# A two-layer transformer on one core: first attention in a new order with its norm in halves, final norm in three groups, the last pair's weight split moved ahead of a rotation

## The chip, the core and the metric

The kernel runs on one core of a Trainium2 chip. The metric is the device time of one execution in microseconds (us); less is better. Five engines work side by side, each through its own queue in order: TensorE (PE in the rows; PEld its weight loads), VectorE (DVE), ScalarE (ACT), GpSimd (POOL) and SyncE (SP), which here only issues DMAs. They wait for each other on semaphores.

## What is computed

Input x has 1024 rows of 512 columns. Four stages follow, each `x = x + f(layernorm(x))`:

```python
x = x + L0_attn(layernorm(x))   # one head of width 128, softmax over all 1024 keys
x = x + L0_ffn(layernorm(x))    # silu(h W1) * (h W3), times W2; each W = base + mean|w - base| * sign(w - base)
x = x + L1_attn(layernorm(x))   # latent attention, 32 heads, keys chosen by a top-128 index, causal
x = x + L1_ffn(layernorm(x))    # x W^T + bias + eight low-rank additions
```

All products are in float32 quality: each operand is split into a rounded part `_h` and the rest `_l`, and three products (l h, h l, h h) are summed.

## The kernel before

The rows stand in eight tiles of 128 (`xt(0)` to `xt(7)`), which stay on chip throughout. Each engine's program is written out by hand; small strings of steps such as `ATT_ORDER` or `PE_ORDER` set its order, and the same name may stand in the strings of several engines, each doing its share of that step.

**A norm.** VectorE takes the statistics of a tile (L1030), makes mean and variance, ScalarE takes the root (L721), VectorE refines its inverse in five small operations (`newton`, L1005) and scales the tile (`norm_scale`, L1046). TensorE transposes it (L1403), ScalarE copies the rounded part out (L725), VectorE subtracts for the rest (`norm_lo`, L1040). The first norm waits for all eight tiles of x, and then goes through all tiles in one pass. The last norm stands behind a meeting of all five engines (`meet`).

**Weights of the feed-forward layer.** 44 chunks come in through a ring of buffers: SyncE loads base and weight (L424, L425), GpSimd subtracts (L563), ScalarE takes sign and absolute value with a sum (L735, L737) and by that frees the slot. The ring has three slots for nine chunks, then four; the fourth is `row_bc`, which until then holds the attention's output bias. The first 28 chunks must be through before the step `O1` of the first attention ends, since the mean of their absolute values is taken there.

**First attention.** TensorE makes queries and keys (four groups of products, steps `u`), then the values of all eight tiles. In `ATT_ORDER`, S(i) is the scores of query tile i: products on TensorE, maximum on VectorE (L1129), exp on ScalarE (L766), there followed by one weight chunk. T(i) is the transpose of its probabilities: TensorE (L1461), two copies on ScalarE (L774), two subtractions on VectorE (L1137). O is the product with the values for four query tiles, Y(i) the output product of a tile and its addition into x (L1149). All four engines follow the same string.

**Head pairs.** The second attention runs 16 pairs of heads. Their weights are prepared ahead: ScalarE rounds (L893), GpSimd makes the rest (`split_pair`, P in `TAIL_ORDER`, L623), SyncE stores them. When all are stored and the first are loaded again, SyncE signals `hd_go`, for which VectorE waits before its first score. M, L (GpSimd) and R (ScalarE) rotate the first pair's queries. In a pair, S is again a score tile (16 of them; VectorE L1349, exp L966), C the reciprocals of two tiles (L1355), GpSimd scales the probabilities (L692), T is one of 24 groups of transposes (L1715, L972, L1361), V0 to V3 the products with the latent values, W the split of their sum (ScalarE L984, GpSimd L701), Y the output products of four row tiles. Each period does half of the row tiles for the pair before and its own; what is left of the last pair comes at the very end (`output`, `LAST_BANKS`), with eight additions and statistics.

**Final layer.** After the meeting: norm of eight tiles, per tile 12 products with the combined matrix `wfin`, bias added on GpSimd (L710), sum on VectorE (L1390), store.

## Time and profile before

| | us |
|---|---|
| median of 3 runs (lowest, highest) | 1475.95 (1475.61, 1476.82) |
| profiled execution, time | 1476.29 |
| profiled execution, span of its records | 1474.5 |
| TensorE busy, share of the span | 1327.4, 90% |
| VectorE busy | 1105.6, 75% |
| ScalarE busy | 832.5, 56% |
| GpSimd busy | 640.5, 43% |

The profile page lists busy time, 40 slices of the span, the chain of work that ended last, and the costliest groups. The trace behind it holds every instruction with its start, length and what ended the idle time before it. Busy shares are a mean over stages with different limits; what a change is worth is read from its own stage.

### The profile page before, as it was taken

The numbers are of one execution on the slowest core, as the hardware profiler recorded it, in microseconds if no ns is written. First come the engines' busy times: TensorE is split into PE (matmuls) and PEld (weight loads), VectorE is DVE, ScalarE is ACT, GpSimd is POOL, SyncE is SP. The second block draws the span as 40 slices with busy tenths as digits, with TensorE's granted clock in tenths as the row PEclk, the third lists the DMA queues.
The fourth block names the chain that finished last, engine by engine and source line by source line (L and its number), as shares of the span: only waits on it lengthen the run. The fifth ranks groups of instructions, "written<-read, shape, count | busy, mean of one in ns | idle before, by whom it ended". The sixth has DMA issues, their size and how long they took to land.

```text
span 1474.5 us, 21228 instructions
## 1 busy us (share of the span) xinstructions
PE 1327.4 (90%) x7144; PEld 1105.3 (75%) x7144; DVE 1105.6 (75%) x2233; ACT 832.5 (56%) x1813; POOL 640.5 (43%) x629
## 2 busy tenths in 40 slices
PE   2777999999989789998659999999999999999977
PEld 1656788888789677776348888888888888888866
DVE  5637434433548599999969998898898998898864
ACT  4554442222236556774557767666676767667631
POOL 3421120000027445645556555655666555555522
PEclk9978999999999999998669999999999999999988
DMA  6531220000022334754820000000000000000101
GB/s 217 177 100 51 70 81 0 1 19 1 17 81 64 102 75 122 227 181 140 269 95 14 1 28 28 28 28 28 28 16 12 28 27 28 28 27 15 51 29 58
DMA packets 83722, 95.59 MB, mean 65 GB/s; under 512 B 11680, under 2 KB 59296, under 8 KB 83104
## 3 DMA queue, kind: packets, MB, share of 16 engines
q1 hardware_dynamic: 83616, 94.24, 20.2%
q8 instruction: 59, 0.97, 0.3%
q14 instruction: 47, 0.39, 0.1%
HBM read 75.34 MB, written 18.87 MB: 64 GB/s over the span
## 4 chain that ended last, share of the span: by engine, by line
PE 68%; DVE 18%; ACT 4%; issue 4%; DMA 2%; POOL 2%; SPq 1%; DVEq 1%; ACTq 0%; POOLq 0%
PE ps L328 16%; PE ps L330 15%; PE ps L329 15%; PE ps L1715 8%; PE ps L1735 3%; DVE acc L1299 3%; PE ps L1734 3%; DVE top L1310 2%; DVE xn_l L1361 1%; DVE rop L1322 1%; DVE acc L1313 1%; DVE rop L1320 1%; DVE pm L1349 1%; DVE rop L1321 1%; PE ps L1430 1%
## 5 line engine op out<-in xcount | busy, mean ns | idle before, releaser
L692 POOL TENSOR_SCALAR pm<-pm,smx 128x128 f32<-128x128 f32 (+7 forms) x256 | 190.5, 753 | 214.6 <-DVE smx L1355 214.6
L966 ACT ACTIVATE pm<-pm,smx 128x128 f32<-128x128 f32 (+7 forms) x256 | 197.2, 772 | 39.8 <-DVE smx L1349 38.7
L1349 DVE CUSTOM_DVE_ANT_0 pm<-ps,mbias 128x128 f32<-128x128 f32 (+7 forms) x256 | 191.3, 752 | 34.0 <-PE ps L1715 13.1
L1715 PE MATMUL ps<-ident,pm 128*128 128x128 f32 x1152 | 176.2, 278 | 9.0 <-DVE xn_l L1361 3.5
L972 ACT ACTIVATE xn_h<-ps 128x512 fp32r<-128x512 f32 (+3 forms) x256 | 128.8, 513 | 86.0 <-PE ps L1715 82.9
L1361 DVE TENSOR_TENSOR xn_l<-ps,xn_h 128x512 fp32r<-128x512 f32 (+3 forms) x256 | 144.6, 587 | 26.6 <-ACT xn_h L972 25.6
L328 PE MATMUL ps<-latT_l,qc_h 128*128 128x512 f32 (+3 forms) x384 | 143.1, 373 | 20.5 <-DVE smx L1349 12.5
L1715 PEld LDWEIGHTS ps<-ident,pm 128*128 128x128 f32 x1152 | 133.4, 142 | 35.3 <-issue 12.3
L330 PE MATMUL ps<-latT_h,qc_h 128*128 128x512 f32 (+3 forms) x384 | 134.1, 349 | 0.0
L329 PE MATMUL ps<-latT_h,qc_l 128*128 128x512 f32 (+3 forms) x384 | 133.4, 347 | 0.0
L1299 DVE SCALAR_TENSOR_TENSOR acc<-ps,iw,acc 128x768 f32<-128x768 f32 (+4 forms) x105 | 87.1, 876 | 23.5 <-ACT ps L865 23.3
L328 PEld LDWEIGHTS ps<-latT_l,qc_h 128*128 128x128 f32 x384 | 73.2, 191 | 37.4 <-DVE smx L1349 13.0
L1734 PE MATMUL ps<-xn_l,v 128*128 128x512 f32 (+3 forms) x256 | 92.7, 368 | 1.6 <-DVE xn_l L1361 1.6
L659 POOL TENSOR_TENSOR rop<-rop 128x512 f32<-128x512 f32 x60 | 77.3, 1288 | 36.2 <-DVE rop L1322 36.2
L328 PE MATMUL ps<-xn_l,wc 128*128 128x512 f32 x224 | 91.7, 409 | 0.0
L1313 DVE MATCH_REPLACE8 acc<-top,acc 128x640 f32<-128x640 f32 (+4 forms) x112 | 89.7, 809 | 0.0
L330 PE MATMUL ps<-xn_h,wc 128*128 128x512 f32 x224 | 89.3, 398 | 0.0
L329 PE MATMUL ps<-xn_h,wc 128*128 128x512 f32 x224 | 89.2, 398 | 0.0
L563 POOL TENSOR_TENSOR wring<-wring,base 128x512 f32<-128x512 f32 (+1 forms) x36 | 47.8, 1332 | 95.3 <-DMA wring<-in_L_ffn_w 95.1
L1735 PE MATMUL ps<-xn_h,v 128*128 128x512 f32 (+3 forms) x256 | 88.4, 364 | 0.0
L865 ACT ACTIVATE ps<-ps 128x640 f32<-128x640 f32 (+4 forms) x112 | 74.0, 690 | 24.8 <-PE ps L330 24.5
L1310 DVE MAX8 top<-acc 128x8 f32<-128x640 f32 (+4 forms) x112 | 85.8, 813 | 0.1
(280 smaller groups left out, 3699.1 us busy)
## 6 DMA issues: line engine op xcount, KB each, us to landing
iwq_raw<-in_L_attn_idx_wq_w SPq DMA_DIRECT2D x48, 256.0 KB, 3.2
base<-in_L_ffn_mean_w SPq DMA_DIRECT2D x28, 256.0 KB, 2.8
wring<-in_L_ffn_w SPq DMA_DIRECT2D x24, 256.0 KB, 3.0
ow_raw<-in_L_attn_o_w SPq DMA_DIRECT2D x8, 512.0 KB, 3.9
xn_t<-in_L_attn_o_w SPq DMA_DIRECT2D x8, 512.0 KB, 4.0
wuvo<-pr_even SPq DMA_DIRECT2D x8, 512.0 KB, 4.9
wuvo<-pr_hl SPq DMA_DIRECT2D x8, 512.0 KB, 4.8
wuvo_h<-wuvo SPq DMA_DIRECT2D x16, 256.0 KB, 2.6
```

The lines of the kernel that those rows point to most:

```text
L328: pe.matmul(dst, lh, rl, start=start, stop=False)
L329: pe.matmul(dst, ll, rh, start=False, stop=False)
L330: return pe.matmul(dst, lh, rh, start=False, stop=stop)
L692: pool.tensor_scalar(pm[:, i % 4, 0:w], pm[:, i % 4, 0:w], smx[:, 32 + i:33 + i], 0.0, ALU.mult, ALU.add).then_inc(hd_p, 1)
L966: act.activation(pm[:, i % 4, 0:w], pm[:, i % 4, 0:w], ACT.Exp, bias=smx[:, i:i + 1], scale=-1.0, accum_out=smx[:, 16 + i:17 + i]).then_in ...
L972: act.activation(dst[:, 4 * c:4 * c + nk, tile(tq % 4)], ps[:, 4 + i % 2, 0:nk * P].rearrange("p (k s) -> p k s", k=nk), COPY).then_inc(hd ...
L1299: dve.scalar_tensor_tensor(acc_of(t), score(n, t), w, acc_of(t), ALU.mult, ALU.add)\
L1349: dve.tensor_tensor_reduce(out=pm[:, i % 4, 0:w], in0=two_banks(2 * (i % 2), w), in1=mbias[:, TRI[t]:TRI[t + 1]], scale=1.0, scalar=3.0 * BIG,
L1361: dve.tensor_tensor(dl[at], ps[:, 4 + i % 2, 0:nk * P].rearrange("p (k s) -> p k s", k=nk), f(dh[at]), ALU.subtract).then_inc(hd_lo, 1)
L1715: done = pe.transpose(ps[:, 4 + i % 2, tile(k)], pm[:, tq % 4, tile(4 * c + k)], ident[:])
L1734: pe.matmul(ps[:, 6, q], v, pl[:, k, q], start=k == 0, stop=False)
L1735: done = pe.matmul(ps[:, 6, q], v, ph[:, k, q], start=False, stop=k == nk - 1)
```

## The change

*First attention.* x's two halves have a semaphore each, and norm statistics, root and scales are done by halves (`first_norm`). The raw weights and the bias have buffers of their own (`attn_raw`, `bo_bc`), which overlap the third base buffer; chunks from 28 on wait until these have been read. The ring has four slots from the start. The split of the weight matrix is cut into four pieces between the second half's tiles; wo's split (W) and the bias additions (B) stand later. The value tiles (V) stand behind S1, their bias comes by a one-row product, their rounded part is copied by ScalarE. Each engine has a string of its own.

*Head start.* `P15` stands ahead of `M3`; ScalarE's `R3` stands behind the last mask conversions.

*End.* A period of its own for the last pair (`LAST_PE` and its like): A(i) is the previous pair's output product of row tile i, B(i) the last pair's, both ahead of V3; P15 is reciprocal and scale of the last query tile on VectorE; W0 stands behind T20 on ScalarE, not behind T22. The meeting is gone. The norm runs over tiles 0-1, 2-3, 4-7; tiles 6 and 7 are scaled on GpSimd.

```diff
-    _slot = _c % 3 if _c < ROW_FREE else (_c - ROW_FREE) % 4
+    _slot = _c % 4
-              "P8 F0 F1 P9 F2 F3 P10 P11 M0 P12 L0 M1 P13 L1 M2 P14 L2 M3 P15 L3".split()]
+              "P8 F0 F1 P9 F2 F3 P10 P11 M0 P12 L0 M1 P13 L1 M2 P14 L2 P15 M3 L3".split()]
-             "S0 S1 S2 T0 S3 T1 S4 T2 S5 T3 S6 O0 T4 Y0 Y1 S7 Y2 T5 Y3 T6 T7 O1 Y4 Y5 Y6 Y7".split()]
+ATT_PE = items("S0 S1 V0 V1 V2 V3 S2 V4 V5 V6 V7 T0 S3 T1 S4 T2 S5 T3 S6 O0 T4 S7 Y0 Y1 T5 Y2 T6 Y3 T7 O1 "
+               "Y4 Y5 Y6 Y7")
+ATT_ACT = items("S0 S1 C2 V0 C2 S2 C1 V1 T0 C1 T1 S3 T2 S4 C1 T3 S5 C1 S6 C3 O0 T4 C1 S7 T5 C1 T6 C1 T7 O1")
+ATT_DVE = items("S0 S1 W0 V0 S2 B0 V1 T0 S3 T1 S4 T2 S5 T3 S6 B4 O0 T4 S7 Y0 Y1 T5 Y2 T6 Y3 T7 O1 Y4 Y5 Y6 Y7")
+LAST_PE = """T9 S11 T10 V0 S12 T11 T12 S13 T13 V1 T14 S14 T15 S15 T16 T17 V2 T18 T19 A0 T20 A1 T21 A3 T22 T23 A2
+    B0 B1 B2 B3 V3"""
+LAST_DVE = """C4 S10 T8 T9 T10 S11 T11 V0 S12 T12 C5 S13 C6 T13 V1 T14 S14 T15 S15 C7 T16 T17 P15 T18 V2 T19 T20 T21
+    T22 T23"""
+LAST_ACT = """T10 T11 V0 T12 S11 S12 S13 T13 V1 T14 T15 S14 T16 T17 S15 T18 V2 T19 T20 W0 T21 T22 T23"""
+LAST_POOL = "S8 S9 S10 S11 S12 S13 S14 W0"
...
+            def first_norm(half):
+                c = slice(4 * half, 4 * half + 4)
+                dve.wait_ge(ld_x[half], 64)
+                for t in range(4 * half, 4 * half + 4):
+                    dve.bn_stats(stats[:, 6 * t:6 * t + 6], xt(t))
...
+            for t in range(4, NT):
+                norm_scale(0, t)
+                norm_lo(0, t - 1)
+                if t == 4:
+                    dve.wait_ge(ld_a, 80)
+                split(wqkv_h[:, t - 4, :], wqkv_l[:, t - 4, :], raw[:, t - 4, :])
...
+                if kind == "S":
+                    if i == 0:
+                        pe.wait_ge(at_qkv, 4)
...
+            pe.wait_ge(hd_x, 4 * (PAIRS - 1) + 2)
+            norm_tile(3, 0)
+            norm_tile(3, 1)
+            last_product(0)
             pe.wait_ge(hd_olo, 2 * PAIRS)
-            for i in range(4):
-                output(4 + i, PAIRS - 1, LAST_BANKS[i], False, True)
-            meet(pe, 1)
+            for t in range(4, NT):
+                products(t, PAIRS - 1, SUM_BANKS[t], True, True).then_inc(hd_y, 1)
+            norm_tile(3, 2)
+            norm_tile(3, 3)
+            last_product(1)
+            last_product(2)
+            last_product(3)
+            norm_tile(3, 4)
+            norm_tile(3, 5)
+            for t in range(4, NT):
+                last_product(t)
+                if t < 6:
+                    norm_tile(3, t + 2)
```

ScalarE's queue of before in the steps S3 to T2 of the first attention (`p` is the exp's output, `sgn` and `wring` or `row_bc` a weight chunk, `xn_h` the copies of the transposed probabilities):

```order
L766 ACTIVATE p,sm<-ps,sm 128x1024
L735 ACTIVATE sgn<-row_bc 128x512
L737 ACTIVATE row_bc,absum<-row_bc 128x512
L774 ACTIVATE xn_h<-ps 128x4x128 x2
L766 ACTIVATE p,sm<-ps,sm 128x1024
L735 ACTIVATE sgn<-wring 128x512
L737 ACTIVATE wring,absum<-wring 128x512
L774 ACTIVATE xn_h<-ps 128x4x128 x2
```

And the same engine now, from T0 to T3:

```order
L823 ACTIVATE xn_h<-ps 128x4x128 x2
L771 ACTIVATE sgn<-row_bc 128x512
L773 ACTIVATE row_bc,absum<-row_bc 128x512
L823 ACTIVATE xn_h<-ps 128x4x128 x2
L809 ACTIVATE p,sm<-ps,sm 128x1024
L823 ACTIVATE xn_h<-ps 128x4x128 x2
L809 ACTIVATE p,sm<-ps,sm 128x1024
L771 ACTIVATE sgn<-wring 128x512
L773 ACTIVATE wring,absum<-wring 128x512
L823 ACTIVATE xn_h<-ps 128x4x128 x2
```

Before, a chunk stood between each exp and the copies of the tile before; now copies and exps follow each other, with fewer chunks between.

GpSimd's queue of before at the last pair of the weight preparation (`pr_hl` is the split, the three rows ahead of it are M3, `qc_l` is L2 and L3):

```order
L666 TENSOR_TENSOR qc_l<-rop,qc_h 128x512
L678 TENSOR_TENSOR rop<-rop,cosq 128x512
L679 TENSOR_TENSOR rop<-rop,sinq 128x512
L682 TENSOR_TENSOR rop<-rop 128x512
L623 TENSOR_TENSOR pr_hl<-pr_out,pr_hl 128x1024
L666 TENSOR_TENSOR qc_l<-rop,qc_h 128x512
```

The same place now:

```order
L685 TENSOR_TENSOR qc_l<-rop,qc_h 128x512
L642 TENSOR_TENSOR pr_hl<-pr_out,pr_hl 128x1024
L697 TENSOR_TENSOR rop<-rop,cosq 128x512
L698 TENSOR_TENSOR rop<-rop,sinq 128x512
L701 TENSOR_TENSOR rop<-rop 128x512
L685 TENSOR_TENSOR qc_l<-rop,qc_h 128x512
```

The split stands three operations earlier.

TensorE's queue of before at the last transposes of the last pair (`ident,pm`), with the last row of V2 ahead and the first of V3 behind:

```order
L1735 MATMUL ps<-pTa_h,v3 128x128
L1715 MATMUL ps<-ident,pm 128x128 x21
L1734 MATMUL ps<-xn_l,v3 128x512
```

The same place now, down to A3 (`wuvo` rows are output products, three of them for each of A0, A1, A3):

```order
L1871 MATMUL ps<-pTa_h,v3 128x128
L1851 MATMUL ps<-ident,pm 128x128 x6
L345 MATMUL ps<-wuvo_l,ol_h 128x512
L346 MATMUL ps<-wuvo_h,ol_l 128x512
L347 MATMUL ps<-wuvo_h,ol_h 128x512
L1851 MATMUL ps<-ident,pm 128x128 x4
L345 MATMUL ps<-wuvo_l,ol_h 128x512
L346 MATMUL ps<-wuvo_h,ol_l 128x512
L347 MATMUL ps<-wuvo_h,ol_h 128x512
L1851 MATMUL ps<-ident,pm 128x128 x3
```

Output products stand between the groups of transposes, where 21 transposes stood in a row.

## Rows read from the trace of the kernel before

**Rows 1.** The page: its span, and the chain that ended last by engine.

```profile
span 1474.5 us, 21228 instructions
...
PE 68%; DVE 18%; ACT 4%; issue 4%; DMA 2%; POOL 2%; SPq 1%; DVEq 1%; ACTq 0%; POOLq 0%
```

**Rows 2.** Windows: length, five engines' busy time (count), TensorE clock, DMA share, GB/s.

```profile
4.00:5.00 1.00, 0.00 (x0) 0.00 (x0) 0.00 (x0) 0.00 (x0) 0.00 (x0) 1.00 0.90 303
```

**Rows 3.** Timeline from the start: start, length, engine, line, operation, count, idle before.

```profile
0.73 3.71 SPq L396 DMA_DIRECT2D x<-in_L_attn_x  x8
...
9.40 4.84 DVE L1030 BATCH_NORM_STATS2 stats<-x 128x6 f32<-128x512 f32 x8 [9.40 <-DMA x<-in_L_attn_x]
...
15.20 3.91 POOL L563 TENSOR_TENSOR wring<-wring,base 128x512 f32<-128x512 f32 x3 [13.51 <-DMA wring<-in_L_ffn_w]
...
27.49 1.51 DVE L1046 TENSOR_SCALAR xn_t<-x,mv,rs_out 128x512 f32<-128x512 f32 x1
...
42.79 4.90 DVE L1073 TENSOR_TENSOR x<-x,row_bc 128x512 f32<-128x512 f32 x8
...
42.85 0.77 PE L328 MATMUL ps<-xn_l,wqkv_h 128*128 128x512 f32 x1 [9.63 <-DVEq L1071]
```

**Rows 4.** TensorE in the first attention (timeline), and the window 68 to 128.

```profile
56.56 0.22 PE L328 MATMUL ps<-wqkv_l,xn_h 128*128 128x128 f32 x1
...
67.23 0.45 PE L328 MATMUL ps<-qkT_l,qkT_h 128*128 128x512 f32 x1
...
76.30 1.91 PE L1461 MATMUL ps<-ident,p 128*128 128x128 f32 x8
...
101.28 0.79 PE L328 MATMUL ps<-xn_l,v_h 128*128 128x512 f32 x1 [4.09 <-DVE xn_l L1137]
...
127.49 0.80 PE L328 MATMUL ps<-xn_l,v_h 128*128 128x512 f32 x1 [1.41 <-DVE xn_l L1137]
...
68.00:128.00 60.00, 38.44 (x149) 29.46 (x148) 29.51 (x49) 37.61 (x71) 19.38 (x16) 0.76 0.36 118
```

**Rows 5.** One step of the first attention on ScalarE and VectorE (timelines).

```profile
84.18 1.12 ACT L766 ACTIVATE p<-ps,sm 128x1024 f32<-128x1024 f32 x1 [2.23 <-DVE sm L1131]
...
87.01 1.08 ACT L774 ACTIVATE xn_h<-ps 128x512 fp32r<-128x512 f32 x2
...
87.64 1.29 DVE L1137 TENSOR_TENSOR xn_l<-ps,xn_h 128x512 fp32r<-128x512 f32 x2 [3.50 <-ACT xn_h L774]
88.85 1.21 DVE L1129 TENSOR_REDUCE sm<-ps 128x1 f32<-128x1024 f32 x1
```

**Rows 6.** The start of the heads: ScalarE, GpSimd, VectorE (timelines).

```profile
742.54 1.06 ACT L893 ACTIVATE pr_hl<-pr_out 128x1024 fp32r<-128x1024 f32 x1
...
747.45 2.36 POOL L623 TENSOR_TENSOR pr_hl<-pr_out,pr_hl 128x1024 fp32r<-128x1024 f32 x1
...
754.55 0.29 DVE L1349 CUSTOM_DVE_ANT_0 pm<-ps,mbias 128x128 f32<-128x128 f32 x1 [6.10 <-issue]
```

**Rows 7.** The end: the window 1411 to 1425, then timelines of four engines.

```profile
1411.00:1425.00 14.00, 10.45 (x40) 8.20 (x41) 4.69 (x9) 5.20 (x11) 3.38 (x3) 0.63 0.01 2
...
1411.37 0.19 ACT L966 ACTIVATION_READ_ACCUMULATOR pm<-pm,smx 128x1 f32 x1
...
1411.85 2.11 POOL L692 TENSOR_SCALAR pm<-pm,smx 128x896 f32<-128x896 f32 x2 [4.90 <-DVE smx L1355]
...
1418.87 0.79 PE L1734 MATMUL ps<-xn_l,v 128*128 128x512 f32 x1 [1.56 <-DVE xn_l L1361]
...
1440.34 0.20 DVE L1009 RECIPROCAL rs_out<-rs_sqrt 128x8 f32<-128x8 f32 x1 [1.64 <-ACT rs_sqrt L721]
...
1441.59 1.00 DVE L1046 TENSOR_SCALAR xn_t<-x,mv,rs_out 128x512 f32<-128x512 f32 x2
...
1442.29 1.94 PE L1403 MATMUL ps<-ident,xn_t 128*128 128x128 f32 x8 [9.08 <-DVE xn_t L1046]
...
1449.15 0.60 PE L1403 MATMUL ps<-ident,xn_t 128*128 128x128 f32 x4
...
1470.86 0.40 PE L330 MATMUL ps<-qc_h,xn_h 128*128 128x512 f32 x1
```

More of the change, by code:

```diff
@@ L989, in _ @@
                 head_period(period)
-            meet(act, 1)
-            sqrt(6, NT)
-            for t in range(NT):
+            act.activation(table[:, 3:4], ones[:, 0:1], ACT.Sqrt)
+            sqrt(6, 2)
+            sum_half(PAIRS - 1, 3)
+            norm_hi(3, 0)
+            sum_hi(PAIRS - 1, 1)
+            norm_hi(3, 1)
+            sqrt(7, 2, 2)
+            norm_hi(3, 2)
+            norm_hi(3, 3)
+            sqrt(8, 4, 4)
+            for t in range(4, NT):
                 norm_hi(3, t)
@@ new lines, in half_norm @@
+                rsqrt(k, n, first)
+            raw = attn_raw[:, 0:NK * 3 * D0].rearrange("p (k n) -> p k n", k=NK)
+            def first_norm(half):
+                c = slice(4 * half, 4 * half + 4)
+                dve.wait_ge(ld_x[half], 64)
+                for t in range(4 * half, 4 * half + 4):
+                    dve.bn_stats(stats[:, 6 * t:6 * t + 6], xt(t))
+                dve.drain()
+                for t in range(4 * half, 4 * half + 4):
+                    dve.bn_aggr(mv[:, t, :], stats[:, 6 * t:6 * t + 6])
+                dve.drain()
+                dve.tensor_scalar(rs_var[:, c], mv[:, c, 1], EPS, None, ALU.add)
+                dve.drain().then_inc(at_rv, 1)
+                dve.wait_ge(at_rs, half + 1)
+                root(4, 4 * half)
@@ L1074, in _ @@
-            dve.drain().then_inc(row_free, 1)
             for u in range(4):
@@ L1080, in _, with values @@
                 dve.drain().then_inc(at_qkv, 1)
-            for b in range(2):
-                dve.wait_ge(at_proj, 5 + b)
-                tmp = xn_t[:, b, :].rearrange("p (k s) -> p k s", k=4)
-                for i in range(4):
-                    dve.tensor_tensor(tmp[:, i, :], ps[:, 4 + b, tile(i)], bv_bc[:], ALU.add)
-                dve.drain()
-                split(v_h[:, 4 * b:4 * b + 4, :], v_l[:, 4 * b:4 * b + 4, :], tmp)
-                dve.drain().then_inc(at_v, 1)
+            def values(b):
+                dve.wait_ge(at_vhi, b + 1)
+                dve.tensor_tensor(v_l[:, 4 * b:4 * b + 4, :], ps[:, 6 + b, :].rearrange("p (k s) -> p k s", k=4),
+                                  f(v_h[:, 4 * b:4 * b + 4, :]), ALU.subtract).then_inc(at_v, 1)
             def means(m, a, b):
@@ L1113, in row_stats @@
                 dve.bn_stats(stats[:, 6 * i:6 * i + 6], xt(i))
-            for kind, i in ATT_ORDER:
+            for kind, i in ATT_DVE:
+                if kind == "V":
+                    values(i)
+                    continue
+                if kind == "W":
+                    split(wo_h[:], wo_l[:], attn_raw[:, NK * 3 * D0:])
+                    dve.drain().then_inc(at_w, 1)
+                    continue
+                if kind == "B":
+                    for t in range(i, i + 4):
+                        dve.tensor_tensor(xt(t), xt(t), bo_bc[:], ALU.add)
+                    dve.drain().then_inc(at_b, 1)
+                    continue
                 if kind == "O" and i == 1:
@@ L1393, in _ @@
+            last_add(6)
+            last_stats(6)
+            last_add(7)
+            last_stats(7)
+            half_norm(8, 4, 4)
+            norm_scale(3, 4)
+            norm_scale(3, 5)
+            dve.drain().then_inc(en_rs, 1)
+            for t in range(NT):
+                if t < 4:
+                    norm_lo(3, t + 4)
+                last_out(t)
         @block.tensor
@@ L1682, in _, with products, output @@
                         queries(0, i)
-            def output(i, p, bank, first, last):
-                for q in ((p - 1, p) if not first and not last else (p,)):
-                    one = mm3(pe, ps[:, bank, :], ol_h[:, q % 2, tile(i)], ol_l[:, q % 2, tile(i)],
-                              wuvo_h[:, q % 2, :], wuvo_l[:, q % 2, :], q == p - 1 or first or last, q == p)
-                one.then_inc(hd_y, 1)
+            def products(i, q, bank, start, stop):
+                return mm3(pe, ps[:, bank, :], ol_h[:, q % 2, tile(i)], ol_l[:, q % 2, tile(i)],
+                           wuvo_h[:, q % 2, :], wuvo_l[:, q % 2, :], start, stop)
+            def output(i, p, bank):
+                if p:
+                    products(i, p - 1, bank, True, False)
+                products(i, p, bank, p == 0, True).then_inc(hd_y, 1)
             def head_period(period):
-                for kind, i, p in steps(PE_ORDER, period):
+                for kind, i, p in steps(LAST_PE if period == PAIRS - 1 else PE_ORDER, period):
                     if kind == "S":
```

341 lines of the change are left out of this document (203 added, 138 removed).

## The prediction

> **What bounds the kernel now.** I read the page's chain of work first [rows 1]: TensorE holds 68% of it and VectorE 18%, so over most of the span a cheaper instruction elsewhere gains nothing. The change touches neither the feed-forward weights nor fifteen of the sixteen head pairs, so I looked only at the stretches that it rewrites: the first attention (0 to 150 us), the start of the heads (743 to 755 us) and the end (from 1411 us).
>
> At the start VectorE waits until 9.40 us for all eight row tiles of x. The roots and scales that follow share their time with GpSimd's weight differences: a scale of one row tile that meets one takes 1.51 us, where two that meet none take 1.00 [rows 3, 7]. TensorE begins its projections at 42.85 us, when all of VectorE's weight splits are done. The 48 projection products take until 56.56 us, and the 96 narrow products of the values until 67.23 us, when the first scores begin [rows 3, 4].
>
> From there to 127.49 us, where the second output product begins [rows 4], no engine is full. A step repeats every 6.15 us, and it is a ring through two in-order queues [rows 5]: exp at 84.18, 1.3 us with its accumulator; one weight chunk (sign and abs) of 1.4 to 1.5 us, until the copies at 87.01; then ScalarE's first copy of the transposed probabilities, 0.6 us; VectorE's two subtractions 1.29 us; only behind them the next maximum, 1.21 us and some 0.3 us to the next exp. VectorE's queue holds T(i) ahead of S(i+1), and ScalarE's holds S(i) and a chunk ahead of T(i), though the scores of S(i+1) have long been computed.
>
> At the head start VectorE ends its top-k work at 748.45 us and takes the first score at 754.55. The signal that it waits for comes behind the last pair's store, and that store behind GpSimd's split, which starts at 747.45 though its input was complete at 743.60 [rows 6].
>
> At the end TensorE waits for the last probabilities, runs the last value product V3 at the lower of its two levels (granted clock 0.63 over 1411 to 1425), ends 36 output products at 1433.2, stands idle for 9.08 us until 1442.29 and ends at 1471.3 [rows 7]. That idle time is eight additions with statistics on VectorE, a meeting of all engines, a table load and the root.
>
> **Prices.** From 1449.15 to 1471.26 stand 84 wide products and 24 transposes [rows 7]; with 0.11 us a transpose, as a narrow product costs 10.67/96 [rows 4], a wide product is 0.23 us. The 48 projections took 13.7 us where 48 x 0.23 is 11.0, so one restart from the 1.2 GHz level costs 2.7 us. A VectorE root takes 1.25 us (1440.34 to 1441.59), a scaled row tile 0.5, statistics of a tile 0.6 (4.84/8) [rows 3, 7]. The three changes are far apart in time, with bound stretches between, so their gains add.
>
> **Part 1, the first attention.** *Halves.* Cumulating the 303 KB/us of DMA traffic from 2.0 us [rows 2], 1.05 MB are through at 5.4; with the 1.1 us by which the signal for all of x came behind its bytes, the first half is there at 6.5 (bounds: that, and 9.4 if the tiles land together). Four statistics, root and scales follow, the first scale at 11.1 instead of 19.45. GpSimd now has four ring slots free at once and works from 15.2 to 20.4. The second half's root ends at 22.0, after four tiles whose ring (scale, transposes, copy, subtraction) takes about 1.4 to 2 us each. The weight split is cut into four pieces of 0.4 + 0.55 us set between tiles 4 to 7, wo's split and the eight additions of the bias (4.90 us) go behind the scores. By hand the last subtraction ends at 31.8. To it I add collisions: a scale that met GpSimd took 1.51 us, not 0.5 [rows 3]; two of these make 33.5. Bounds: none 31.8; four and the late landing 38. Projections thus start 9.3 us earlier.
>
> No row shows VectorE's statistics beside a busy GpSimd, and the second four (17.3 to 19.7) will meet it. I take them at 0.6; were all four blocked like the scale, 4 us more, which the upper bound holds. The Trainium skill, SBUF — State Buffer, "SBUF: two separate sides", has the shared port pair as an exclusive lock that a VectorE instruction takes only in a two-port mode or with two SBUF inputs; by that rule statistics, with one input, would not be blocked. It speaks against the split pieces (a copy, and a subtraction of two SBUF inputs) set beside GpSimd's chunks: by it each of the eight could wait for one 1.3 us difference, half of it on average, and the projections would start at 37 instead of 33.5, the time being 3.5 us longer. The scale's 1.51 us agrees with the rule; no row here shows statistics beside GpSimd.
>
> *A new wait.* The scores S0 now stand straight behind the projections, ahead of the value tiles. TensorE ends the fourth projection at 33.5 + 13.7 = 47.2, ScalarE copies (0.7), VectorE splits (1.3), so S0 starts at 49.3 where the values used to hide that. Behind the 2 us wait I charge a restart: S0 and S1 take 5.1 us, to 54.4. Values V0 to V3 (5.8 us with the new bias product, which replaces four VectorE additions), S2 (1.4) and V4 to V7 (5.8) bring TensorE to 67.4, which is T0's start. Meanwhile the first three exps and five chunks run beside it. T0 began at 76.30 before: 9 us gained so far.
>
> *The steps.* ScalarE's new queue takes T(i) ahead of S(i+2), and its chunks no longer stand in each step. Hand-walking all three queues with the durations above gives T1 at 69.7, T2 at 72.1, T3 at 74.7 and the first output product at 78.8 (101.28 before). It ends at 84 to 87; ScalarE reaches it at 86.3, held by exp S6 and three chunks. Then T4 at 87, S7's exp at 91.5, T5 92, T6 94.1, T7 to 98.4 and its last subtraction at 100.2. ScalarE's own content from T0 is 8 x 1.08 + 5 x 1.3 + 9 chunks x 1.4 + 1.2 = 29 us, so 33 us is close to what that queue allows. I take 101.0 with a little lower clock: gain **26.5** (127.49 to 101.0). Bounds: 31 with no restart; if the lower level rules half of the steps (T + S costs 4.4 us there against 2.35) and the ring of two copies sets each step at 4.5 us, 18; with the late landing as well, 14. Behind this point the order is the old one.
>
> **Part 2, head start.** The split of the last pair moves ahead of the three rotation operations M3 (3.7 us). It waits for ScalarE's 743.60 and, behind L2, starts at 743.7 and ends at 746.05. Store, loads and drain are unchanged at 4.74 us (749.81 to 754.55), so VectorE starts at 750.8, behind its own 748.45. The table load of exp now stands behind R3, which waits for M3 (749.9), and ends near 751.9, so the first exp comes 0.8 us later behind its score than before; the first reciprocals have that slack. Gain **3.5**, bounds 2 (exp counts in full, and the two stores touch) and 3.75.
>
> **Part 3, the end.** The reciprocal and scale of the last query tile move to VectorE: exp ends at 1411.56, P15 is 1.2 us (1.00 as for two 512-column scales, plus a reciprocal), so it is done at 1412.8, against 1413.96 on GpSimd. The price: T18's subtraction and V2's addition wait behind it, and W0, now behind T20 on ScalarE, waits for that addition until 1414.25. So T21 to T23 are copied from 1414.9 and V3's input is complete at 1417.3. TensorE fills the gap: the output products of tiles 0, 1 and 3 (2.1 us) among the transposes, then A2 and B0 to B3 (3.5 us) from 1415.85 to 1419.3, then V3 at the full level, 3.0 us, to 1422.3 (some 1424.5 before, 36 products ahead of 1433.2). Here the filled gap must keep the clock up; if not, 2.7 us.
>
> Next the norm in groups of 2, 2 and 4. Tiles 0 and 1 have their sums at 1418.1 and 1419.4, their root at 1422.3, and the first scale at 1422.9. The last half-sum, tile 1's scale, the addition of tile 2 and tile 0's low part share VectorE, so the first final product starts at 1425.6. That gap has 1.2 us of work in 3.3, as the one before V3 had, so I charge a restart (2.7). Then 12 + 12 products (5.5), transposes of tiles 2 and 3 (0.9) and 36 products (8.25) run to 1442.95; the last four tiles' sums, statistics, root and first scale end at 1442.6 beside it, so little wait is left: tile 4's transposes, copy and low part end at 1445.0. The remaining 48 products and the 8 transposes of tiles 6 and 7 are 11.9 us, so TensorE ends at 1457.0, against 1471.26. Store and last addition behind it stay 3.25. Gain **14.3**. Bounds: 16.5 with no restart; 8 with restarts at V3 and again at tile 4.
>
> **Sum.** 26.5 + 3.5 + 14.3 = 44.3. The profiled execution took 1476.29 with a span of 1474.5; it gives 1432.0, and as the median of the runs shown is 0.34 lower, **1431.7 us**.
>
> **Rivals.** (1) *The lower clock and the queue ring keep half of the steps' gain.* For it: the mean granted clock over the old steps is 0.76, half of 68 to 128 us at the lower level [rows 4]. Against: gaps shrink. Attention then gives 14 instead of 26.5: 1444. (2) *The halves of x land together and GpSimd collides at every piece.* The start loses 4 us: 1435.5. (3) *The clock stays at its upper level*, since all three gaps are shorter: 2.7 at S0, 2.7 at the final norm, 2 in the steps: 1424.5. (4) *Slower: the weight ring becomes the bound.* A slot's round trip is issue 0.8, landing 3.0, difference 1.3, sign and abs 1.4 = 6.5 us, for four slots 1.6 us a chunk, and 28 chunks must be through before the second output product. It decides from (101 - 17.7)/28 = 3.0 us a chunk, a round trip of 12. If loads that now collide with more chunks in a row made it 19, chunks would end at 150.7 and the kernel, 23.2 behind the old point with 17.8 of other gains, at 1481, slower. The highest DMA share seen leaves no room for a threefold landing. (5) *The change doesn't do what it says*, an engine waiting for another's moved signal so that all stays as it was: 1476.
>
> **How the numbers follow.** Forecast 0.60, rival 1 0.18, rival 2 0.10, rival 3 0.08, rival 4 0.03, rival 5 0.01. The range 1422.5 to 1447 takes in rivals 1 to 3 and leaves out the tails of their bounds. A measurement of this kernel can tell 0.2% (3 us) from no change: faster 0.96, same 0.01, slower 0.03.
>
> **What would show it.** Right: the projections start near 33.5 us, the second output product near 101, VectorE's first score of the heads some 4 us less behind its last top-k replacement (2.4 us, not 6.1), V3 behind five product blocks, and TensorE's idle time between 1433 and 1442 gone. Wrong: ScalarE waiting for GpSimd's differences in the steps, a granted clock of 0.5 over most of 50 to 100 us, or TensorE idle for over 3 us ahead of tile 4's transposes.

## The result, and the profile after

The changed kernel takes **1443.72 us** (median of 4 runs, 1442.61 to 1445.15) against 1476.38 before: a ratio of 0.978, with a 95% interval of 0.976 to 0.980. The forecast was 1431.7 with a range of 1422.5 to 1447.0: the sign and the range held, and the time came out 12 us above the forecast. The profiled execution took 1442.61 us with a span of 1440.8, so the span lost 33.7 us where 44.3 were forecast.

```profile
span 1440.8 us, 21299 instructions
PE 71%; DVE 16%; ACT 4%; issue 3%; DMA 2%; POOL 1%; SPq 1%; DVEq 0%; ACTq 0%
```

The chain of work is TensorE's and VectorE's as in [rows 1]. Cut at the two points that the prediction used, the second output product and VectorE's first score, the 33.7 us come from these places:

| stretch | before, us | after, us | gain | forecast |
|---|---|---|---|---|
| to the second output product | 127.49 | 113.43 | 14.1 | 26.5 |
| from there to VectorE's first score | 627.06 | 623.55 | 3.5 | 3.5 |
| from there to the end of the span | 719.95 | 703.8 | 16.1 | 14.3 |

The miss lies in the first attention, 12.4 us short; the last stretch gave 1.8 more than forecast. TensorE's timeline of the changed kernel there (start, length, line, operation, output and inputs, count, idle time before and who ended it):

```profile
33.17 0.77 PE L345 MATMUL ps<-xn_l,wqkv_h 128*128 128x512 f32 x1 [2.17 <-DVEq L1143]
49.68 0.50 PE L345 MATMUL ps<-qkT_l,qkT_h 128*128 128x512 f32 x1 [2.71 <-DVEq L1149]
...
52.62 0.48 PE L1539 MATMUL ps<-bv_bc,ones 1*128 1x128 f32 x2
54.52 0.48 PE L1539 MATMUL ps<-bv_bc,ones 1*128 1x128 f32 x2
...
67.52 0.79 PE L1539 MATMUL ps<-bv_bc,ones 1*128 1x128 f32 x2
...
71.00 0.79 PE L1539 MATMUL ps<-bv_bc,ones 1*128 1x128 f32 x2
...
77.81 1.93 PE L1584 MATMUL ps<-ident,p 128*128 128x128 f32 x8
...
113.43 0.80 PE L345 MATMUL ps<-xn_l,v_h 128*128 128x512 f32 x1 [1.41 <-DVE xn_l L1214]
```

The projections start at 33.17 us (forecast 33.5, before 42.85), and S0 at 49.68 (49.3). But the transposes T0, forecast at 67.4 and at 76.30 before [rows 4], start at 77.81: the 9 us gained at the start are lost in the value tiles. L1539 is the product of one row of ones with the bias row that opens each value tile. A tile has 12 other products of 0.111 us, 1.33 us; it takes 1.90 (52.62 to 54.52), so the bias product costs 0.57 us where I charged 0.11. At the end a tile takes 3.48 us (67.52 to 71.00). The windows of the same stretch show why (us; then the busy time and instructions of PE, PEld, DVE, ACT and POOL; the granted clock; DMA share; GB/s):

```profile
50.00:54.00 4.00, 4.00 (x23) 3.14 (x21) 2.51 (x3) 3.74 (x7) 0.80 (x2) 1.00 0.73 230
54.00:58.00 4.00, 4.00 (x32) 3.62 (x32) 3.07 (x3) 3.62 (x8) 3.72 (x3) 1.00 0.49 167
58.00:62.00 4.00, 4.00 (x20) 3.71 (x20) 0.00 (x0) 1.43 (x5) 1.43 (x2) 0.61 0.77 241
...
74.00:78.00 4.00, 4.00 (x18) 3.66 (x18) 0.00 (x0) 0.00 (x0) 0.00 (x0) 0.50 0.02 4
```

The granted clock is 1.00 to some 58.8 us, then 0.5, the 1.2 GHz level, for 24 us, **while TensorE is busy all the time**: PE shows 4.00 of 4.00 us in each of these windows. Ahead of every fall in the profile of before TensorE had been idle a few microseconds earlier.

The start was as forecast. VectorE's second four statistics take 2.46 us, 0.6 each, with GpSimd's differences running from 15.63 to 20.86 beside all of them; what meets GpSimd and does wait is the split of q and k behind the projections, 1.62 to 1.68 us a subtraction instead of 0.69:

```profile
15.63 3.94 POOL L582 TENSOR_TENSOR wring<-wring,base 128x512 f32<-128x512 f32 x3 [13.95 <-DMA wring<-in_L_ffn_w]
17.34 2.46 DVE L1120 BATCH_NORM_STATS2 stats<-x 128x6 f32<-128x512 f32 x4
...
46.61 1.68 DVE L1086 TENSOR_TENSOR qkT_l<-xn_t,qkT_h 128x512 fp32r<-128x512 f32 x1
...
48.90 0.69 DVE L1086 TENSOR_TENSOR qkT_l<-xn_t,qkT_h 128x512 fp32r<-128x512 f32 x1
```

At the head start VectorE's first score comes 1.4 us behind its last top-k replacement, where it came 6.1 us behind before [rows 6]; the table load of exp (737.34) is now what the first exp waits for. At the end TensorE fills the gap ahead of V3, and the 9.08 us of idle time of [rows 7] are gone:

```profile
729.84 2.35 POOL L642 TENSOR_TENSOR pr_hl<-pr_out,pr_hl 128x1024 fp32r<-128x1024 f32 x1
734.41 1.21 DVE L1390 MATCH_REPLACE8 acc<-top,acc 128x1024 f32<-128x1024 f32 x1
736.98 0.29 DVE L1429 CUSTOM_DVE_ANT_0 pm<-ps,mbias 128x128 f32<-128x128 f32 x1 [1.36 <-issue]
...
1394.63 0.75 DVE L1442 TENSOR_SCALAR pm<-pm,smx 128x1024 f32<-128x1024 f32 x1
1398.72 1.29 DVE L1449 TENSOR_TENSOR xn_l<-ps,xn_h 128x512 fp32r<-128x512 f32 x2 [0.38 <-ACT xn_h L1030]
...
1402.02 0.39 PE L1870 MATMUL ps<-xn_l,v 128*128 128x512 f32 x1
...
1408.63 0.47 PE L345 MATMUL ps<-qc_l,xn_h 128*128 128x512 f32 x1 [0.71 <-DVE xn_l L1097]
...
1425.36 0.50 PE L345 MATMUL ps<-qc_l,xn_h 128*128 128x512 f32 x1 [0.98 <-DVE xn_l L1097]
```

V3 (from 1402.02) and the final products (from 1408.63) run at the upper level: no window behind 1388 us shows less than 1.00.

### The profile page after: what moved, and what is told of

It reads as the page before. It is cut to its first block, busy times and chain, and to the rows that moved or that the text cites. A ratio compares the mean times of both kernels' runs of the same rounds, so it can differ in the third digit from the quotient of the medians.

```text
span 1440.8 us, 21299 instructions
## 1 busy us (share of the span) xinstructions
PE 1329.5 (92%) x7160; PEld 1107.8 (77%) x7160; DVE 1107.4 (77%) x2247; ACT 832.9 (58%) x1819; POOL 641.7 (45%) x630
## 4 chain that ended last, share of the span: by engine, by line
PE 71%; DVE 16%; ACT 4%; issue 3%; DMA 2%; POOL 1%; SPq 1%; DVEq 0%; ACTq 0%
PE ps L345 17%; PE ps L347 16%; PE ps L346 16%; PE ps L1851 9%; PE ps L1871 3%; PE ps L1870 3%; DVE acc L1376 3%; DVE top L1387 2%; DVE xn_l L1449 1%; DVE rop L1399 1%; DVE acc L1390 1%; DVE rop L1397 1%; DVE pm L1429 1%; DVE rop L1398 1%; PE ps L1551 1%
## 5 line engine op out<-in xcount | busy, mean ns | idle before, releaser
L717 POOL TENSOR_SCALAR pm<-pm,smx 128x128 f32<-128x128 f32 (+1 forms) x255 | 188.8, 749 | 208.5 <-DVE smx L1436 208.5
L582 POOL TENSOR_TENSOR wring<-wring,base 128x512 f32<-128x512 f32 (+1 forms) x33 | 43.1, 1309 | 108.4 <-DMA wring<-in_L_ffn_w 108.1
L345 PE MATMUL ps<-ikT_l,iqT_h 128*128 128x512 f32 (+3 forms) x176 | 66.1, 376 | 23.3 <-DVE acc L1376 22.1
```

Of the source, the lines that this page charges most:

```text
L345: pe.matmul(dst, lh, rl, start=start, stop=False)
L717: pool.tensor_scalar(pm[:, i % 4, 0:w], pm[:, i % 4, 0:w], smx[:, 32 + i:33 + i], 0.0, ALU.mult, ALU.add).then_inc(hd_p, 1)
```

## The experiments

All build on the changed kernel, or on it with one edit, as said. They were taken on several chips, each beside the kernel of before, whose medians there were 1474.6 to 1476.4 us and whose single runs reached from 1470.0 to 1479.0; so a difference of 1 or 2 us between medians below says little by itself. Two theories were open on the 10.4 us that T0 came late. **A:** the bias products bring the clock down, beside their own price. **B:** the 2.7 us wait ahead of S0 does, and the products only cost their time.

### No bias product

```diff
 def value_tile(t):
     dst = ps[:, 6 + t // 4, tile(t % 4)]
-    pe.matmul(dst, ones[0:1, :], bv_bc[0:1, :], start=True, stop=False)
     for k in range(NK):
         last = mm3(pe, dst, xn_h[:, k, tile(t)], xn_l[:, k, tile(t)],
-                   wqkv_h[:, k, tile(2)], wqkv_l[:, k, tile(2)], False, k == NK - 1)
+                   wqkv_h[:, k, tile(2)], wqkv_l[:, k, tile(2)], k == 0, k == NK - 1)
```

> Leaves out the bias of the values: the product of one row of ones with the bias row, that opened each value tile, is gone, and the tile's first real product opens it; nothing else is changed. In the changed kernel a value tile took 1.90 us at the upper level (12 narrow products are 1.33), the clock fell at 58.7 us, and the first transposes T0 came at 77.8 us. Theory A, the bias products bring the clock down: eight times 0.57 us go and the clock stays up, S0 and S1 2.9, V0 to V3 5.3, S2 1.4, V4 to V7 5.3 behind 49.7 give T0 at 64.6, 13 us earlier; kernel 1430.5 to 1433. Theory B, the 2.7 us wait ahead of S0 brings it down and the products only cost their own time: the fall stays near 58.7, T0 comes near 71, kernel 1437 to 1439.

Measured 1429.56 us (1428.14 to 1431.64), a ratio of 0.969 (0.966 to 0.971) to before. T0 starts at 68.64, not at 64.6, because the wait ahead of S0 was 5.0 us in this run and the clock was low behind it until some 57 us; from there it stays at 1.00 up to 101. The time is below theory A's figure, and theory B's 1437 is out. A wait ahead of S0 does cost a restart, but the clock then comes back.

### The values first

```diff
-ATT_PE = items("S0 S1 V0 V1 V2 V3 S2 V4 V5 V6 V7 T0 S3 ...
+ATT_PE = items("V0 V1 V2 V3 S0 S1 S2 V4 V5 V6 V7 T0 S3 ...
```

> TensorE computes the value tiles V0 to V3, bias products and all, ahead of the first scores S0, so that they fill the 2.7 us in which it waited for the split of q and k; every other queue is as in the changed kernel. Theory A, the bias products bring the clock down: the wait goes but the clock still falls within some us of the first value tiles, T0 near 75 instead of 77.8, kernel 1440 to 1442. Theory B, the wait brings it down: no fall, the 19.5 us of S0 to V7 at the upper level stand straight behind 46.9, T0 near 66.5, kernel 1432 to 1434.

Measured 1436.28 us (1433.32 to 1439.79), T0 at 73.09. There is no idle time ahead of the first value tile, and the clock falls all the same, inside V2; it comes back in the scores and falls again inside V6:

```profile
46.00:50.00 4.00, 4.00 (x30) 3.54 (x30) 3.21 (x4) 3.66 (x8) 2.41 (x3) 1.00 0.48 167
50.00:54.00 4.00, 4.00 (x20) 3.61 (x19) 0.00 (x0) 2.21 (x4) 2.18 (x3) 0.56 0.91 284
...
62.00:66.00 4.00, 4.00 (x27) 3.22 (x25) 1.48 (x4) 3.16 (x6) 0.00 (x0) 1.00 0.00 0
66.00:70.00 4.00, 4.00 (x24) 3.69 (x23) 2.37 (x4) 3.58 (x9) 1.26 (x1) 0.69 0.75 235
```

So no wait is needed for the fall. The time lies between the two theories' figures: the values fill the idle time ahead of S0, 2.7 us or more, and the rest of the damage stays.

### Both

> Both of the edits before together: no bias of the values (left out), and V0 to V3 ahead of S0. Under either theory the clock stays up and 14.9 us of products stand straight behind 46.9: T0 near 62, if the first exp, which S0 now releases 5 us later, does not decide; kernel 1428 to 1430. If it gives no more than no bias alone, the first exps and not TensorE set T0.

Measured 1430.25 us (1429.36 to 1433.55): no better than no bias product alone. The clock stays at 1.00 from 46 to 66 us and T0 starts at 64.14, but T1 only at 70.24: TensorE waits 3.64 us for T0's low part on VectorE. With the value tiles cheap, the queues of ScalarE and VectorE set the pace.

### The bias product with 128 rows

```diff
-    pe.matmul(dst, ones[0:1, :], bv_bc[0:1, :], start=True, stop=False)
+    pe.matmul(dst, ident[:], bv_bc[:], start=True, stop=False)
```

> The bias product with 128 rows in place of one: identity times the bias broadcast over all partitions, so the same result, the same float32 operands and the same 128 columns. Theory A in its narrow form, it is the single row (an almost empty array) that brings the clock down: the product costs the same 0.57 us but the clock stays up, T0 near 69.2, kernel 1434 to 1436. If float32 products with their gaps bring it down whatever their rows, or if the wait ahead of S0 does (theory B), all stays at 1443 to 1445 with T0 near 77.8.

```profile
49.03 0.80 PE L345 MATMUL ps<-qkT_l,qkT_h 128*128 128x512 f32 x1 [3.92 <-DVEq L1149]
...
56.52 0.44 PE L1539 MATMUL ps<-bv_bc,ident 128*128 128x128 f32 x2
...
58.08 0.44 PE L1539 MATMUL ps<-bv_bc,ident 128*128 128x128 f32 x2
...
67.28 1.06 PE L1584 MATMUL ps<-ident,p 128*128 128x128 f32 x8
50.00:54.00 4.00, 4.00 (x17) 3.25 (x15) 1.73 (x3) 1.98 (x4) 1.63 (x3) 0.70 0.82 264
54.00:58.00 4.00, 4.00 (x39) 4.00 (x37) 2.98 (x4) 3.27 (x8) 2.56 (x2) 1.00 0.01 5
```

Measured **1432.74 us** (1431.91 to 1434.01), a ratio of 0.971 (0.969 to 0.973). The same bias, again two float32 records to a product and 128 columns, but with all 128 rows of the array filled: a tile takes 1.56 us instead of 1.90 (56.52 to 58.08), so the product costs 0.23 us instead of 0.57, and after the restart behind S0's wait the clock stays at 1.00 to 93 us. T0 starts at 67.28 where the forecast had 67.4, and the second output product at 100.28 where it had 101.0. The edit changes two things at once, the rows and the stationary operand, identity for ones; no run has 128 rows of ones. And of the 13.2 us gained at the second output product the span shows 9.5: what lies behind that point took 1331.0 us here and 1327.4 in the changed kernel.

### The bias product with 32 rows

```diff
-    pe.matmul(dst, ones[0:1, :], bv_bc[0:1, :], start=True, stop=False)
+    pe.matmul(dst, ones[0:32, :], bv_bc[0:32, :], start=True, stop=False)
```

> The bias product of the changed kernel with 32 rows in place of one (the bias is then added 32 times over, so the result differs; the work is the same in kind). Theory A narrow, one row: with 32 rows the clock stays up; the tile takes 1.5 (as with 128 rows) or 1.9 us (as with one row), T0 at 67 to 69, kernel 1432 to 1436. Rival, anything short of the full 128 rows breaks the stream and brings the clock down: T0 near 78, kernel 1443 to 1445.

```profile
57.52 0.48 PE L1539 MATMUL ps<-bv_bc,ones 32*128 32x128 f32 x2
...
59.41 0.48 PE L1539 MATMUL ps<-bv_bc,ones 32*128 32x128 f32 x2
58.00:62.00 4.00, 4.00 (x30) 3.62 (x31) 0.62 (x1) 3.12 (x8) 0.00 (x0) 1.00 0.23 58
62.00:66.00 4.00, 4.00 (x17) 3.62 (x17) 0.69 (x1) 1.67 (x4) 1.49 (x2) 0.51 0.66 204
```

Measured 1443.13 us, with single runs from 1432.06 to 1445.93. The tile takes 1.90 us as with one row (57.52 to 59.41), the clock falls at 62 us, and T0 comes at 80.58. The narrow form of theory A, a single row, falls; what counts on this evidence is a product that leaves part of the rows empty (with ones as its stationary operand, see above). The one run at 1432 suggests that the fall doesn't come, or comes late, in some executions.

### The changed kernel again

> The changed kernel itself, beside the others on this chip. 1443.7 again, within 1.5 us, T0 near 78 us, the clock at its lower level from some 59 us to over 80.

Six runs lie in two groups, 1435.8 to 1438.6 and 1445.5 to 1449.0, median 1442.02. The profiled one is of the lower group: the clock fell only at some 68 us, in the sixth value tile, and T0 came at 75.76. So when the clock falls is open to chance, and the sizes of the edits below are read from the traces, not from medians of so few runs. Over all profiles the pattern is plain. With a bias product of 1 or 32 rows (the changed kernel twice, the values first, the two edits of the heads and the end below, and 32 rows) the clock fell inside the value tiles six times out of six; with 128 rows or none it never fell there in seven. In two of the six, the values first and the head start undone, it fell there twice.

### Halves of x undone

Here and in the next edit the bias product has 128 rows.

```diff
 def first_norm(half):
     c = slice(4 * half, 4 * half + 4)
     dve.wait_ge(ld_x[half], 64)
+    dve.wait_ge(ld_x[1], 64)
```

> The halves of x undone, on top of the bias product with 128 rows (1432.7): VectorE's first statistics wait for all eight row tiles instead of four, all else as in that run. The first statistics came at 6.6 us; they come at 9.5 or so now. If what starts earlier at the front reaches the end in full, the projections start 2 to 3 us later and so does everything behind, 1435 to 1436. Rival, the ring of weight chunks or the exps bound the attention and not its start: within 1 us of 1432.7.

Measured 1436.19 us (1435.50 to 1438.23), 3.5 more. The first statistics start at 9.33 us instead of 6.73, the projections at 35.66 instead of 32.28, T0 at 72.79, the second output product at 105.94 against 100.28. The wait ahead of S0 was 5.17 us in this run. What is gained at the front does reach the second output product, where it has grown from 3.4 us at the projections to 5.7 by a longer wait and restart at S0; of that the span shows 3.1, since the rest took 1328.4 us in this run and 1331.0 in the other. The weight ring is not the bound.

### The exps ahead of the copies

```diff
-ATT_ACT = items("... T0 C1 T1 S3 T2 S4 C1 T3 S5 C1 S6 C3 O0 ...
+ATT_ACT = items("... T0 C1 S3 T1 S4 T2 S5 C1 T3 C1 S6 C3 O0 ...
```

> The order of the steps undone on ScalarE, on top of the bias product with 128 rows (1432.7): the exp of S(i+3) stands ahead of the copies of T(i+1) again, from S3 to S5, with as many weight chunks as in that run; TensorE and VectorE as there. By the prediction the old ring then closes again, copy 0.6, two subtractions 1.3, maximum 1.5, exp 1.3: 4.7 us a step instead of 2.4 for three steps, the first output product 6 to 7 us later than 78.8, kernel 1437 to 1440. Rival, the steps gained from the chunks that left them and not from the order: within 2 us of 1432.7.

```profile
74.12 1.09 ACT L823 ACTIVATE xn_h<-ps 128x512 fp32r<-128x512 f32 x2
74.75 1.29 DVE L1214 TENSOR_TENSOR xn_l<-ps,xn_h 128x512 fp32r<-128x512 f32 x2 [1.97 <-ACT xn_h L823]
...
75.96 1.21 DVE L1206 TENSOR_REDUCE sm<-ps 128x1 f32<-128x1024 f32 x1
77.44 1.11 ACT L809 ACTIVATE p<-ps,sm 128x1024 f32<-128x1024 f32 x1 [2.23 <-DVE sm L1208]
78.74 1.08 ACT L823 ACTIVATE xn_h<-ps 128x512 fp32r<-128x512 f32 x2
```

Measured 1440.05 us (1437.62 to 1443.64), 7.3 more. The ring of the prediction stands in the rows: copies at 74.12, subtractions 74.75, maximum 75.96, exp 77.44, and the next copies at 78.74, a period of 4.62 us against 2.3 to 2.6 between the transposes T0 to T3 with the new order. The first output product starts at 86.86 instead of 78.76.

### The head start undone

```diff
-"... L1 M2 P14 L2 P15 M3 L3"
+"... L1 M2 P14 L2 M3 P15 L3"
```

> The second part undone in GpSimd's queue alone: the split of the last pair stands behind the three rotation operations M3 again, ahead of ScalarE's part of the rotation as before; all else is the changed kernel. By the prediction's second part (3.5 us): the split starts some 3.8 us later, VectorE's first score of the heads comes about 6 us behind its last top-k replacement instead of 1.4, and the kernel takes 3.5 to 4 us more than the changed one, 1447 to 1448. Rival, the gain there came from another place (the cast R3 moved on ScalarE): under 1.5 us more.

```profile
733.42 2.36 POOL L642 TENSOR_TENSOR pr_hl<-pr_out,pr_hl 128x1024 fp32r<-128x1024 f32 x1
734.23 1.21 DVE L1390 MATCH_REPLACE8 acc<-top,acc 128x1024 f32<-128x1024 f32 x1
740.52 0.29 DVE L1429 CUSTOM_DVE_ANT_0 pm<-ps,mbias 128x128 f32<-128x128 f32 x1 [5.09 <-issue]
```

Measured 1446.54 us (1441.26 to 1449.18). The median is 2.8 to 4.5 above the changed kernel's two, but its runs spread over 8 us as the others with one row do. The trace is sharper: the split starts at 733.42 instead of 729.84, and the first score comes 5.1 us behind the last replacement instead of 1.4, 3.7 us. Another pair of profiles would have given another figure: in the twelve other profiles with the new head start the first score comes 0 to 3.3 us behind the last replacement, and the whole stretch from the second output product to the first score takes 619.6 to 626.6 us (mean 623.4), against 627.0 here and 627.1 before. So the head start is worth 3.6 us on average, but single profiles scatter over 7 us.

### The fill at the end undone

```diff
-LAST_PE = """... T22 T23 A2 B0 B1 B2 B3 V3"""
+LAST_PE = """... T22 T23 V3 A2 B0 B1 B2 B3"""
```

> The fill at the end undone: V3 stands ahead of the output products A2 and B0 to B3 instead of behind them; all else is the changed kernel. V3 then starts at 1400.0 when its input is complete instead of at 1402.0, behind an idle stretch of TensorE of some 2 us. By the prediction's third part the fill keeps the clock up and brings the sums of tiles 0 and 1 early: without it V3 or what follows runs at the lower level (2.7 us) and the first final product comes 2 to 5 us later; kernel 2 to 6 us longer, 1446 to 1450. Rival, it is only a permutation of equal work with slack behind it: within 1 us of 1443.7.

```profile
1395.23 1.29 DVE L1449 TENSOR_TENSOR xn_l<-ps,xn_h 128x512 fp32r<-128x512 f32 x2 [0.35 <-ACT xn_h L1030]
1396.57 0.50 PE L1870 MATMUL ps<-xn_l,v 128*128 128x512 f32 x1 [1.57 <-DVE xn_l L1449]
1401.39 0.69 DVE L1412 TENSOR_TENSOR x<-x,ps 128x512 f32<-128x512 f32 x1 [4.88 <-PE ps L347]
1406.88 2.33 PE L1522 MATMUL ps<-ident,xn_t 128*128 128x128 f32 x8 [3.46 <-DVE xn_t L1103]
1409.46 0.76 PE L345 MATMUL ps<-qc_l,xn_h 128*128 128x512 f32 x1 [0.25 <-DVE xn_l L1097]
1406.00:1410.00 4.00, 2.74 (x9) 1.93 (x10) 3.83 (x8) 1.71 (x3) 0.80 (x1) 0.56 0.01 2
```

Measured 1447.97 us (1444.48 to 1453.72). In this run everything at the end lies 3.5 us earlier than in the changed kernel (last copies at 1394.60, there 1398.09). V3 starts 2.0 us earlier by that frame, at 1396.57, and still at the upper level. But the first sum of an output tile comes at 1401.39 instead of at 1396.7, TensorE is idle for 3.46 us ahead of 1406.88, the clock falls, and the first final product starts 4.3 us later than in the changed kernel. From there to the end it takes 33.9 us instead of 32.2. The fill is worth 4.3 us for the sums that come early, none of it in V3. The 1.7 us for the clock can't be laid to the fill alone: with it the clock fell at the same place in five of twelve profiles, the second profile of the changed kernel among them, of which this is a window:

```profile
1403.00:1406.00 3.00, 3.00 (x9) 2.33 (x8) 2.52 (x8) 0.20 (x1) 2.29 (x2) 0.50 0.00 0
```

In those five the way from the first final product to TensorE's next wait took 18.0 to 18.3 us, in the seven others 16.7, without the fill 18.5.

### A better order

```diff
-    pe.matmul(dst, ones[0:1, :], bv_bc[0:1, :], start=True, stop=False)
+    pe.matmul(dst, ident[:], bv_bc[:], start=True, stop=False)
-ATT_PE = items("S0 S1 V0 V1 V2 V3 S2 V4 V5 V6 V7 T0 ...
+ATT_PE = items("V0 V1 V2 V3 S0 S1 V4 S2 V5 V6 V7 T0 ...
-ATT_ACT = items("S0 S1 C2 V0 C2 S2 C1 V1 T0 ...
+ATT_ACT = items("V0 S0 S1 C2 C2 S2 C1 V1 T0 ...
-ATT_DVE = items("S0 S1 W0 V0 S2 B0 V1 T0 ...
+ATT_DVE = items("B0 V0 S0 S1 W0 S2 V1 T0 ...
```

> A version that should beat both kernels. On the changed kernel: the bias product with 128 rows (identity times the broadcast bias), V0 to V3 ahead of S0 and V4 ahead of S2 on TensorE, ScalarE's copy and VectorE's subtraction of the first four value tiles ahead of S0, and the four additions B0 ahead of those, into the time in which VectorE has nothing to do. By the run with 128 rows a value tile takes 1.55 us at the upper level: eight tiles 12.4 and S0 to S2 4.2 behind 46.9 give T0 at 63.5 against 67.3 there, and no restart at S0; the first T1 should no longer wait for B0, as it did (3.6 us) in the run without bias and with the values first. Theory A: 3.5 us less than the 1432.7 of the 128 rows, 1428 to 1430. Rival: behind T0 the steps, the chunks or the second output product are held by VectorE or by ScalarE's chunks, so that it stays at 1431 to 1433.

Measured 1430.61 us (1429.63 to 1432.29), between the two expectations. T0 starts at 64.04, but T1 at 70.31, 3.81 us of it idle: B0 beside GpSimd took 3.59 us and delayed the first maximum, and ScalarE then had five weight chunks to run ahead of T0's copies.

```diff
-ATT_ACT = items("V0 S0 S1 C2 C2 S2 C1 V1 T0 ...
+ATT_ACT = items("V0 C1 S0 S1 C2 S2 C2 V1 T0 ...
-ATT_DVE = items("B0 V0 S0 S1 W0 S2 V1 T0 ...
+ATT_DVE = items("V0 S0 S1 W0 S2 B0 V1 T0 ...
```

> The better order once more, with ScalarE's time filled: there the first maximum came late and ScalarE stood idle for 2.3 us (54.3 to 56.6) ahead of the first exp, then ran five chunks between the exps and T0's copies, so that TensorE, done with T0 at 64, waited 3.8 us for T0's low part. Now one chunk stands ahead of the first exp, four behind it, and the four additions B0 go behind S2's maximum, where VectorE had nothing to do for 7.8 us. If ScalarE's content sets the attention, the 1.5 to 2 us filled come off: second output product at 100 instead of 102.1, kernel 1428 to 1429.5. Rival, a chunk that is loaded later than that only shifts the wait: 1430 to 1431.

```profile
62.63 1.07 PE L1584 MATMUL ps<-ident,p 128*128 128x128 f32 x8
67.31 1.16 PE L1584 MATMUL ps<-ident,p 128*128 128x128 f32 x8 [2.21 <-DVE xn_l L1214]
...
97.85 0.80 PE L345 MATMUL ps<-xn_l,v_h 128*128 128x512 f32 x1 [1.57 <-DVE xn_l L1214]
```

Measured **1427.87 us** (1424.67 to 1429.91), a ratio of 0.968 (0.966 to 0.970): the fastest of all, 14 to 16 us below the changed kernel's two medians. No restart at S0, a granted clock of 1.00 from 46 to 97 us, and the second output product at 97.85. T1 still waits 2.21 us.

## Why the prediction was right or wrong

**The step that failed** is "Values V0 to V3 (5.8 us with the new bias product, which replaces four VectorE additions), S2 (1.4) and V4 to V7 (5.8)". I gave the new product the price of a narrow product, 0.11 us. The profile of before has a row for a float32 product of 128 rows and 128 columns, which I had overlooked (L1675, half of the sum that makes the final layer's matrix):

```profile
683.96 0.39 PE L1675 MATMUL ps<-lBT,lA_sb 128*128 128x128 f32 x2
684.18 0.39 PE L1676 MATMUL ps<-ident,lW_sb 128*128 128x128 f32 x2
```

One such product follows the other every 0.22 us, twice the narrow price and what the run with 128 rows then showed. No row of before shows a product with a single row; that had to be bounded, and the bound had to hold the clock. By the rows of the changed kernel the way from the forecast's T0 to the real one is:

| term | us |
|---|---|
| forecast of T0 | 67.4 |
| S0 later than forecast (49.68, not 49.3) | +0.4 |
| restart at S0 charged and not paid in this run (S0 and S1 take 2.94, not 5.1) | -2.2 |
| bias products, 8 x (0.57 - 0.11), and rounding | +3.6 |
| lower level from 58.7 us on: 77.81 less 69.2, which is 49.68 + 2.94 + 8 x 1.90 + 1.38 for S2, all at the upper level | +8.6 |
| T0 | 77.8 |

The 35.6 us from T0 to the second output product are 2.0 more than forecast (33.0 with 128 rows); T0 and S3 still run at the lower level. 10.4 and 2.0 are the 12.4 us of the first row of the table above. The run with 128 rows bears it out: with this one term near what I had (0.23 instead of 0.11), the kernel takes 1432.7 against the 1431.7 of the forecast. That the two lie 1.0 us apart is partly luck: its projections started 1.2 us earlier than forecast, and it paid restarts at S0 and at the final products that the changed kernel's profile did not pay.

**Rival 1** named the right time, 1444, and the right kind of cause, a lower clock, but at the wrong place. The steps kept their speed (exps at 84.03 and 86.38, 2.35 us apart), and the ring is really gone, as the run with the exps ahead shows. The clock fell ahead of them, in a stretch without a gap. I had charged restarts only behind an idle TensorE, and took the value tiles, the busiest stretch, as safe. That 1443.7 still lies in the stated range is luck: the upper part of the range was there for this rival's mechanism, which did not come.

**Halves.** Right: first half there at 6.6 (6.5), first scale 11.3 (11.1), second root done at 22.3 (22.0), projections 33.17 (33.5). Over the other profiles of the same front they start at 32.0 to 34.0, so two collisions were a fair count. Undone, the halves cost 3.5 us by the medians. As to GpSimd's port, the statistics were not blocked, and up to the projections only two instructions are lengthened as by GpSimd's differences, a scale (1.52 us at 22.41) and one of the eight split pieces (a subtraction of 1.56 at 30.81), so that the 37 us weighed beside did not come. The Trainium skill, SBUF — State Buffer, "SBUF: two separate sides", says that a VectorE instruction in a two-port mode or with two SBUF inputs and a GpSimd instruction shut each other out, whichever starts first. The trace agrees: four statistics took 2.46 us beside a busy GpSimd, three subtractions with two SBUF inputs took 1.62 to 1.68, and the fourth, which had started at 48.90, ahead of GpSimd's next difference (49.10), took 0.69, while that difference took 1.64 instead of 1.27.

**The wait at S0.** Its mechanism was right, its size too small: 2.0 forecast, 2.7 to 5.2 measured; in the changed kernel's profile three of the four subtractions of that split wait for weight differences on GpSimd. The restart that I charged was paid in seven of the nine profiles with this order.

**The steps.** Right: T0 to the second output product takes 33.0 us in the run with 128 rows (33.6), 51.2 before.

**The head start.** Right on average: 3.5 us; undone, 3.7. That the first profile gives exactly 3.5 is luck, since this stretch alone varies by 7 us between profiles.

**The end.** 16.1 instead of 14.3, inside its bounds. P15, V3's input and the fill came as forecast (0.1 to 0.4 us off in the old frame). I charged a restart ahead of the first final product (2.7 us); the clock stayed up through gaps of 0.38, 0.99 and 0.71 us, against me 0.8 us elsewhere. This too is luck: behind the same gaps it fell in five of the twelve profiles with the fill, and cost 1.3 to 1.6 us there, not 2.7; their last stretch took 704.5 to 706.4 us, in the seven others 703.6 to 704.6. That the filled gap must keep the clock up isn't shown: V3 ran at the upper level even without the fill, and behind it the clock fell with and without.

## What to carry to other kernels

A new form of an operation has no price until a row shows one: look through the whole trace for its type and size, not only in the stretch that changes, and where there is none bound it by the worst that its neighbours may suffer, the clock of the whole stretch among it, not by the cheapest row of the same width. A product that fills only some rows of the array (a rank-one bias, a broadcast by ones) can be written with all rows, as identity times the value already broadcast; here that alone is worth 9 to 11 us. And when TensorE's share of a stretch is full, read its granted clock before calling the stretch safe.
